# Window numbers read into registers in small portions behind long operations, instead of 16 or 32 at a time

## The reference, cut to what matters

```
src, dst : (100000,) int32, dst sorted
for l in 0, 1, 2, 3:
    h = maximum(layernorm(x), 0)
    x = x + layer_l(h, edge attributes of l, src, dst)
```

```
xs = f_s[edge_src];  w = silu(edge_scalars @ fcW1) @ fcW2         # layers 1 and 2, scalings left out
edge_feat = concatenate([wA * xs * y0, wD * dot(xv, y1), wB * xs * y1, wC * xv * y0])
agg = segment_sum(edge_feat, edge_dst, num_segments=n)

alpha = exp(a - amax[dst]) / den[dst]                              # layer 3
agg = segment_sum(alpha * h, dst, num_segments=n)
```

## Time and profile before

| | |
|---|---|
| median of three runs | 7312.9 us |
| the profiled execution's own time | 7304.86 us |
| its span, from the first instruction to the last | 7302.9 us |
| mean granted clock of TensorE | 0.946 |
| TensorE busy | 6765.1 us (93%) |
| VectorE busy | 6302.5 us (86%) |
| GpSimd busy | 4759.4 us (65%) |
| ScalarE busy | 3832.9 us (52%) |

### The profile page before, as it was taken

One profiled execution on the slowest core, in us unless ns is written; L12 is line 12 of the kernel. 1 busy time (PEld: TensorE's weight loads), 2 busy tenths in 40 slices (PEclk: granted clock), 3 DMA queues, 4 the chain that ended last, 5 costly groups with the idle time before them and its releaser, 6 DMA issues. The chain is left out here.

```text
span 7302.9 us, 114744 instructions
## 1 busy us (share of the span) xinstructions
PE 6765.1 (93%) x33584; PEld 4545.9 (62%) x33584; DVE 6302.5 (86%) x17360; ACT 3832.9 (52%) x10286; POOL 4759.4 (65%) x3558
## 2 busy tenths in 40 slices
PE   6999999997799999989999993899999999998488
PEld 3544454444555555555555562788888888887366
DVE  6999999996599888868888874799999999998795
ACT  3555555553333333343333341677777777776485
POOL 2888888885277777737777753777777777775000
PEclk7999999998699999989999995899999999999798
DMA  8999999999322222212222221444444444443363
GB/s 232 177 176 175 177 177 176 176 175 190 93 63 65 64 65 66 60 37 69 68 69 69 68 50 45 94 96 97 97 98 97 97 96 96 97 97 79 96 191 100
DMA packets 555482, 786.66 MB, mean 108 GB/s; under 512 B 94513, under 2 KB 406231, under 8 KB 554615
## 3 DMA queue, kind: packets, MB, share of 16 engines
q0 software_dynamic: 326592, 425.23, 35.5%
q1 hardware_dynamic: 224038, 353.46, 15.9%
q10 hardware_dynamic: 4240, 0.64, 0.1%
HBM read 472.16 MB, written 306.82 MB: 107 GB/s over the span
## 5 line engine op out<-in xcount | busy, mean ns | idle before, releaser
L675 POOL DMA_INDIRECT fore<-node_table,src_i x1664 | 1727.8, 1038 | 647.9 <-issue 500.1
L1625 DVE TENSOR_TENSOR work<-work 128x128 f32<-128x128 f32 (+6 forms) x4942 | 2012.0, 433 | 54.2 <-DMA work<-src_sum 29.8
L789 POOL DMA_INDIRECT fore<-src_table,put_i x784 | 1357.6, 1732 | 450.2 <-ACT fore L1116 269.7
L742 POOL DMA_INDIRECT src_sum<-work,put_i x832 | 1328.6, 1597 | 400.8 <-issue 182.1
L1377 PE MATMUL bank<-work 128*128 128x384 f32 (+1 forms) x3328 | 1206.6, 506 | 17.3 <-DVE work L1625 17.0
L1377 PEld LDWEIGHTS bank<-work 128*128 128x128 f32 x3328 | 607.0, 192 | 700.1 <-issue 293.9
L948 ACT ACTIVATE work<-bank 64x512 f32<-64x512 f32 x416 | 246.1, 592 | 1433.8 <-PE bank L1344 1433.8
L1625 DVE TENSOR_TENSOR work<-work,bank 128x384 f32 (+6 forms) x2080 | 896.2, 431 | 77.3 <-issue 67.9
L1329 PE MATMUL bank<-work 128*128 128x480 f32 x1664 | 767.9, 595 | 2.2 <-DVE work L1625 1.9
L1358 PEld LDWEIGHTS bank<-w_fc,work 64*128 64x128 f32 x3328 | 532.9, 188 | 237.5 <-issue 225.4
L1358 PE MATMUL bank<-w_fc,work 64*128 64x192 f32 x3328 | 656.3, 338 | 5.4 <-ACT work L948 5.4
(11 more groups left out here) (280 smaller groups left out, 12825.9 us busy)
## 6 DMA issues: line engine op xcount, KB each, us to landing
edge_h<-work SPq DMA_DIRECT2D x196, 320.0 KB, 2.3
work<-edge_h SPq DMA_DIRECT2D x196, 320.0 KB, 3.4
work<-keys SPq DMA_DIRECT2D x196, 256.0 KB, 6.0
fore<-in_dst_row SPq DMA_DIRECT2D x196, 256.0 KB, 3.6
fore<-node_table,src_i POOLq DMA_INDIRECT x1664, 2.7
work<-in_edge_attr SPq DMA_DIRECT2D x196, 128.0 KB, 6.0
src_sum<-work SPq DMA_DIRECT2D x4, 6240.0 KB, 38.0
work<-src_sum SPq DMA_DIRECT2D x100, 240.0 KB, 4.4
```

Of the source, the lines that this page charges most:

```text
L675: return pool.indirect_dma_start(dst, None, table, bass.IndirectOffsetOnAxis(ap=idx, axis=0), bounds_check=bound, oob_is_err=True)
L742: pool.indirect_dma_start(src_sum[t], bass.IndirectOffsetOnAxis(ap=put_i[:, e:e + 1], axis=0), E.run[:, g % 2, t * 480:(t + 1) * 480], Non ...
L789: pool.indirect_dma_start(T.rows[:, b, t, :], None, src_table, bass.IndirectOffsetOnAxis(ap=put_i[:, e:e + 1], axis=0), compute_op=ALU.add ...
L1625: return V_.tensor_tensor(o, p, q, op)
```

## The change

TensorE holds 3 registers instead of 16. In layer 0 it reads 2 numbers in every group. In the first pass of layer 3 it reads 3 numbers at each even h, that is once in a group, ahead of the wait for `dst_turned`. On VectorE, `window` no longer reads; `windows_from(u, n=8)` reads 8 numbers, and is called in layers 1 and 2 in every fourth group behind the 128 x 768 product, and in the second pass in every fourth group behind the 128 x 640 product, with one read of a single number ahead of that loop. The numbers read and the adds and matmuls that use them are the same.

```diff
--- before.py
+++ after.py
@@ -1292,16 +1292,15 @@
                 return stage
 
             table = fore[:, 0:SLOTS * DIM].rearrange("p (j c) -> p j c", c=DIM)
-            held = [pe.alloc_register(f"pe_held{i}") for i in range(16)]
+            held = [pe.alloc_register(f"pe_held{i}") for i in range(3)]
 
             def window_rows(u):
 
                 if u >= UNITS:
                     return table[:, u - UNITS + 1, :]
-                if u % 16 == 0:
-                    n = min(16, UNITS - u)
-                    pe.load(held[0:n], window_i[0:1, u:u + n])
-                window = pe.snap(held[u % 16], min_val=0, max_val=WINDOWS - 1)
+                if u % 2 == 0:
+                    pe.load(held[0:2], window_i[0:1, u:u + 2])
+                window = pe.snap(held[u % 2], min_val=0, max_val=WINDOWS - 1)
                 return table[:, bass.ds(window, 1), :].rearrange("p o c -> p (o c)")
 
             def rows_by_dst(g):
@@ -1489,17 +1488,15 @@
 
                 def dst_rows(h):
                     g, at = h // 2, h % 2 * 2
-                    if h % 8 == 0:
-                        n = min(16, TILES - 2 * h)
-                        pe.load(held[0:n], tile_window_i[0:1, 2 * h:2 * h + n])
                     if at == 0:
+                        pe.load(held[0:3], tile_window_i[0:1, 2 * h:2 * h + 3])
 
                         pe.wait_ge(s.dst_turned, g + 1)
                     if h:
 
                         pe.wait_ge(s.gd_out, h)
                     for t in range(2):
-                        window = pe.snap(held[(2 * h + t) % 16], min_val=0, max_val=WINDOWS - 1)
+                        window = pe.snap(held[at + t], min_val=0, max_val=WINDOWS - 1)
                         last = nc.tensor.matmul(gd[:, t * DIM:(t + 1) * DIM], T.turned[:, g % 2, at + t, :],
                                                 skip[:, bass.ds(window, 1), 0:DIM].rearrange("p o c -> p (o c)"),
                                                 start=True, stop=True)
@@ -1955,12 +1952,15 @@
                 acc = acc_view(l)
                 if u >= UNITS:
                     return acc[:, u - UNITS + 1, :]
-                if u % 32 == 0:
-                    n = min(32, UNITS - u)
-                    windows[0:n] = hold(window_i[0:1, u:u + n], WINDOWS - 1)
-                return acc[:, bass.ds(windows[u % 32](), 1), :].rearrange("p o f -> p (o f)")
-
-            windows = [None] * 32
+                return acc[:, bass.ds(windows[u](), 1), :].rearrange("p o f -> p (o f)")
+
+            windows = {}
+
+            def windows_from(u, n=8):
+
+                n = min(n, UNITS - u)
+                if n > 0:
+                    windows.update(zip(range(u, u + n), hold(window_i[0:1, u:u + n], WINDOWS - 1)))
 
             own_tiles = [dve.alloc_register(f"dve_tile{i}") for i in range(8)]
 
@@ -2079,6 +2079,8 @@
                     tt(t2, t1[:, :, 0, :], t1[:, :, 1, :], ALU.add).then_inc(dve_own, c.step())
                     dve.wait_ge(dve_own, parts + 1)
                     tt(blocks[:, :, :, 0:S], bc(t0, 2, 3), bc(yy[:, :, 1:4], 3, S), ALU.mult).then_inc(dve_own, c.step())
+                    if g % 4 == 1:
+                        windows_from(2 * g - 2)
                     dve.wait_ge(dve_own, parts + 2)
                     tt(t2, t2, t1[:, :, 2, :], ALU.add).then_inc(dve_own, c.step())
                     if g >= 2:
@@ -2534,10 +2536,13 @@
 
                     dve.wait_ge(s.p2_spread, g + 1)
                     tt(in_planes(P2.msg[:, b, :, 0:160]), in_planes(P2.h[:, g % DEPTH]), bc(P2.spread[:, b], 2, 5), ALU.mult).then_inc(s.p2_messages, 1)
+                    if g % 4 == 2:
+                        windows_from(2 * g - 3)
                     if g >= 2:
 
                         dve.wait_ge(s.p2_added, 2 * g - 3)
                         add3(2 * g - 3)
+                windows_from(0, 1)
                 unrolled(ALL_GROUPS, [(0, weigh)])
                 for u in range(2 * ALL_GROUPS - 4, 2 * ALL_GROUPS):
```

## The result

The changed kernel takes 7351.95 us (median of 7 runs, 7337.03 to 7380.29) against 7310.67 us of the kernel before (7 runs, 7295.02 to 7318.77). The ratio is 1.0061, with a 95% interval of 1.0044 to 1.0077: slower by 0.6%, where 1.1% faster was predicted. The profiled execution took 7357.44 us, with a span of 7355.6 us and a mean granted clock of 0.945; that is 52.7 us more span than before.

A forecast was written before the change was run, and what follows sets the result against it. TensorE was taken to bound four of five edge stages, VectorE the second pass of layer 3. Gains of 1 + 25.3 + 25.4 + 30.2 = 81.9 us off 7312.9 gave 7231 us, range 7219 to 7252.

The forecast's parts named there:

- the price of a load: All register loads: time linear in count, 63 ns a register and 97 ns beside, from loads of 8, 16 and 32.
- Part 4: Second pass, VectorE: 13 loads become 49 of 8 and one of 1, nearly hidden behind the product; gain 30.2 us.
- Part 3: First pass of layer 3, TensorE: 49 loads of 16 become 196 of 3, all hidden; gain 25.4 us.
- part 2: Layers 1 and 2, VectorE: 13 loads each become 49 of 8, hidden behind the product; gain 25.3 us.
- part 1: Layer 0, TensorE: 25 loads of 16 become 196 of 2, covered; gain 1 us, bounds 0 to 3.
- cover of 0.58 us: First pass, TensorE: part of a load hidden by work issued before, 1.107 - 0.53 = 0.58 us.
- Rival C: Something else paces a stage once stalls are gone, VectorE in first pass or edge rows' DMA in second; 7259 us, chance 0.06.
- the 1.57 us found there: Layer 0, TensorE: a load of 16 lasting 1574 ns cost its group almost nothing, so 1.57 us counts as covered.
- B: TensorE loads: a load of 3 takes what one of 8 does, 0.6 us; 7235 to 7236 us, chance 0.06.
- A: Second pass: loads begin only with the product, leaving 0.21 us exposed 49 times; 7240 us, chance 0.13.
- D: TensorE: any load empties it, slower from 0.21 us exposed per load over 392 loads; 7384 us, chance 0.015.
- E: Stalls remain because they come from the wait beside the load; within 2 us of 7313, chance 0.015.

The follow-up runs named there:

- experiment 3: Changed kernel with the second pass's 8-number loads started at a multiple of eight, two register sets in turn; 7296.51 us, ratio to before 0.9989.
- experiments 2 and 6: Changed kernel reading four numbers, not three, in the first pass (ratio 1.0055); one gather of four left out, old loads (first pass 2191.6 us) and aligned (2164.6).
- experiments 7 and 9: Kernel with every load aligned, but first-pass loads of 16 numbers for its first 32 groups (7244.53 us) or first eight groups (7247.57 us).
- probe: Kernel before plus 20 unused loads on TensorE and 23 on VectorE; the trace has none of them; 7327.18 us in one run.
- experiment 6: One gather of four left out in layers 1, 2 and first pass, from kernel before (layer 1 1112.8 us) and from kernel with every load aligned (1099.4).
- p2_aligned: The kernel of experiment 3: changed kernel with second-pass loads of 8 started at a multiple of eight; 7296.51 us, ratio 0.9989.
- ladder: Kernel with every load aligned plus twenty used VectorE loads of varied count and start between layer 3's passes; 3 numbers took 741 ns, 4 took 348.
- switch_16: Kernel with every load aligned, but only the first two loads of the first pass (first eight groups) of 16 numbers; 7247.57 us, ratio 0.9908.
- all_aligned: Changed kernel with every load of whole fours: four numbers in first pass and layer 0, second pass started at multiples of eight; 7274.17 us, ratio 0.9953.
- p1_four: Changed kernel reading 4 numbers a group instead of 3 in the first pass of layer 3; 7336.8 us, ratio 1.0055.
- aligned_fewer: Kernel with every load aligned, one gather of four left out in layers 1, 2 and first pass; one run, first pass 2164.6 us, layer 1 1099.4.
- p1_switch: Kernel with every load aligned, but the first pass reads 16 numbers at a time in its first 32 groups, fours behind; 7244.53 us, ratio 0.9911.

## Why the prediction was wrong

**The step that failed is the price of a load,** in the second paragraph: "What a load of registers takes is linear in their number", 63 ns a register. The loads of the earlier trace rows have 8, 16 and 32 numbers and start at multiples of 8. They show what whole fours from a multiple of four cost (4 x 63 = 250 ns), and say nothing of numbers left over or of an odd start. Both occur in the change: 2 and 3 numbers on TensorE, and 8 from unit 1 on in the second pass. The diff showed it (`2 * g - 3` against `2 * g - 2`), and I read it as a matter of when the load is issued.

- Part 4, second pass: the load was priced at 0.60 us and costs 1.845. Everything around it held: it starts 0.1 us before the product, and 0.60 fits (experiment 3, 322.0 us against the 323.7 that 353.9 - 30.2 gives). 49 times 1.25 us, 61 us, took the place of the 31 us that went: +30.4 instead of -30.2 us, the largest part of the error (61 us of 135 between -81.9 and +52.7). Part 3 adds 38, part 2 adds 22, and the parts between the stages 17; part 1 takes 3.5 off.
- Part 3, first pass: priced at 286 ns, costs 769. The cover of 0.58 us was right, so 0.19 us stay out in 193 groups where 0.53 in every fourth went, a mean of 0.13: 193 x (10.88 - 10.82) = 12 us slower instead of 25.4 faster. My upper bound for a load of 3, 598 ns "of 8 numbers", rested on the belief that fewer can't cost more.
- Part 3 has a second fault, hidden behind the first: "What is late next? VectorE ... and it is not late". With a cheap load GpSimd is, in 10.85 us a group (experiments 2 and 6). Rival C had the shape, something else that paces a stage, and named the wrong engine; its argument against, three quick groups between two loads, is void: in that trace GpSimd was on its quick way, with 1.4 us to spare in a group, and which way it takes goes with how the pass begins, which the loads change (experiments 7 and 9).
- Part 2: layer 2 went as foreseen, 8.1 us and 1.5 for its first load against 9.5 gained. All traces with the new loads and the usual clock have 1097.3 to 1099.2 us there; with the old ones two have 1106.9 and 1106.8, and probe in its one run 1122.1. In layer 1 the loads' "issue" idle time went (18.5 us to 0.2), and nothing came of it: GpSimd's gathers take 5.43 us a group, and VectorE waits for them 60.0 us instead of 20.2. With one of four gathers left out 13.4 us came (experiment 6), so here too the stalls were priced about right and the next engine was missed.
- Part 1: layer 0's loads of 2 took 906 ns and not 300, covered all the same by the 1.57 us found there. The stage is 4.5 us shorter; p2_aligned, with the same loads there, is another 3.6 us shorter, so this is of the size by which it differs from run to run.
- Rivals: B had the right doubt, that a short load isn't short, at too low a price. The floor of about 600 ns that the Trainium skill gives in "DMA: Bandwidth & Descriptors", section "Latency and other measured facts", isn't what these traces show: 1 number took 0.31 us, 4 took a median of 0.33 in the first pass and 0.35 in the ladder. The Trainium skill, "Runtime: NRT & Kernel Launch", section "Instruction fetch mechanics", gives about 200 ns a register, for loads from HBM. The numbers here come from SBUF; the single ones take 215 to 220, but four in one block take 250 together, so that the figure fits neither 8 nor 32 numbers of the earlier trace rows. A's form, gaps ahead of the add behind the product, is what happened, but with the load's price for a cause and not its start. D's price, 0.21 us exposed for each TensorE load, was nearly met in the first pass (0.19), but not in layer 0, and not for D's cause. E is out: the stalls of 16 and 32 did go.

The range (7219 to 7252) left out the case that happened, because every bound in it took a load's price from rows of the same kind, multiples of eight.

## What to carry to other kernels

Before moving or cutting a register load, look at its count and at where it starts: in these runs only blocks of four numbers from a multiple of four were cheap (250 ns a block, 220 ns for each single number), so read four where three are needed, and shift the batch rather than start it at an odd number. A price taken from rows of one kind, here all multiples of eight, isn't a line for others. And a stage that is quick between its stalls may be so thanks to them: ask of each engine that waits in those groups how much it has to spare, GpSimd's gathers too, and look at the mean over a whole stage when the stalls are gone.

## What the runs showed of the hardware

- A load of registers: about 100 ns, 250 ns for each whole four from a multiple of four, about 220 ns for every single number. It is the same on TensorE (3: 769 ns, 4: 331) as on VectorE (741, 348), and 2.1 us for 32.
- The same adding gather of 128 rows occupies GpSimd for 1.5 to 2.0 us in the quick kernels, and for 3.05 us once in nearly every group of the slow ones (3.65 in a few groups of them). The long ones lie over the score operations of VectorE, all of them with their operands in SBUF. The Trainium skill, "SBUF — State Buffer", section "SBUF: two separate sides", says that VectorE, in an operation with two SBUF inputs, and GpSimd, when it reads SBUF, take one port pair in turns, whoever comes first holding it for the whole instruction. The rows don't decide whether that is the cause. In switch_16 a gather over the same operations is through in 1.77 us, in all_aligned the first score operation starts 0.74 us into the gather of 3.05 and takes its usual 0.42, and no run moved an operand.
- TensorE shows as busy for 10.85 of 10.85 us in p1_four and for 10.69 of 10.69 in aligned_fewer, with the same matmuls: that it looks full didn't tell which engine set the pace.
- In layer 0 the loads of two took from 532 to 1352 ns, with a median of 906; the first pass's loads of three kept within 765 to 830. The DMA engines are busier there (share 1.03 from 400 to 800 us, 0.47 from 5000 to 5400), but that this is the cause isn't shown: with the same code in layer 0 the loads of four have a median of 585 ns in all_aligned and of 340 in p1_switch.
- Open: why the mean gather of layer 1 varies from 1035 to 1069 ns with the same loads, and the layer with it, and what exactly about the fill of the first pass puts GpSimd on its slow way. The quickest kernels with all gathers are p1_switch and switch_16, 0.9% under the kernel before.
